# A first graph layer worked on 128x128 matrices, its one-hots on GpSimd, and matmuls that bridge three waits

## The reference

```
x = x + L0_gnn(layernorm(x), emb_1, emb_2, alpha_p, beta_p, edge_weight, src, dst, 5)

def L0_gnn(inputs, emb_1, emb_2, alpha_p, beta_p, edge_vals, edge_row, edge_col, num_iters):
    x1 = inputs @ emb_1
    x2 = inputs @ emb_2
    sim = softmax(leaky_relu(x1 @ x2.T, 0.2), axis=-1)          # 128 x 128
    vals = edge_vals * sim[edge_row, edge_col]                   # 2048 edges
    normalize = segment_sum(vals, edge_row)[:, None]
    alpha, beta = exp(alpha_p), exp(beta_p)
    denom = beta + normalize * alpha + alpha
    for _ in range(num_iters):                                   # out starts as inputs
        sp = segment_sum(vals[:, None] * out[edge_col], edge_row)
        out = (inputs * beta + (sp + out) * alpha) / denom
    return out
```

## Time and profile before

| what | value |
|---|---|
| median of 3 runs | 586.34 us (583.44 to 587.7) |
| profiled execution, own time | 588.12 us |
| its span | 586.4 us |
| mean granted TensorE clock | 0.988 |
| PE busy | 557.6 us, 95% |
| DVE busy | 492.7 us, 84% |
| ACT busy | 413.9 us, 71% |
| POOL busy | 15.7 us, 3% |
| DMA | 168.06 MB, mean 287 GB/s |

### The profile page before, as it was taken

The page is one execution under the profiler, slowest core; times in us unless marked ns, Lnnn a source line. Parts: engine busy times, 40 slices in busy tenths (PEclk is TensorE's granted clock), DMA queues, the critical chain, the costliest instruction groups (busy, mean ns, idle before and its releaser), DMA issues.

```text
span 586.4 us, 8286 instructions
## 1 busy us (share of the span) xinstructions
PE 557.6 (95%) x2743; PEld 453.6 (77%) x2743; DVE 492.7 (84%) x491; ACT 413.9 (71%) x426; POOL 15.7 (3%) x40
## 2 busy tenths in 40 slices
PE   5898999997999999999999999999998799999997
PEld 4666888885678887688888888888877688888886
DVE  7599989886769986888898998989987769998996
ACT  5777787873259876868778778787852457878783
POOL 3100000000100000000000000000000200000000
PEclk9799999998999999999999999999999999999999
DMA  8579998897257975788989989899873158999920
GB/s 285 210 269 424 373 354 343 331 344 267 72 197 285 357 310 190 265 334 336 355 319 352 354 320 355 334 343 352 330 289 118 72 186 308 349 350 365 344 104 19
DMA packets 26861, 168.06 MB, mean 287 GB/s; under 512 B 5228, under 2 KB 5357, under 8 KB 6856
## 3 DMA queue, kind: packets, MB, share of 16 engines
q1 hardware_dynamic: 25430, 165.72, 75.2%
q10 hardware_dynamic: 1410, 2.07, 1.0%
HBM read 167.51 MB, written 0.26 MB: 286 GB/s over the span
## 4 chain that ended last, share of the span: by engine, by line
PE 77%; DVE 11%; ACT 5%; issue 3%; DMA 2%; POOL 2%; ACTq 0%; POOLq 0%; DVEq 0%
PE y L634 33%; PE pre L634 33%; PE tp L646 5%; DVE w_lo L1022 4%; DMA scal<-in_L_gnn_eps 2%; ACT w_hi L366 2%; PE pre L641 2%; DVE st L969 1%; POOL rstd L324 1%; ACT L439 1%; PE wt L867 1%; DVE XN L989 1%; POOL rstd L323 1%; DVE w_lo L1013 0%; DVE X L1107 0%
## 5 line engine op out<-in xcount | busy, mean ns | idle before, releaser
L1022 DVE TENSOR_TENSOR w_lo<-raw,w_hi 128x2048 fp32r<-128x2048 f32 x151 | 340.1, 2287 | 48.7 <-ACT w_hi L366 48.3
L366 ACT ACTIVATE w_hi<-raw 128x2048 fp32r<-128x2048 f32 x152 | 285.4, 1915 | 0.0
L444 ACT ACTIVATE hT_hi<-tp 128x512 fp32r<-128x512 f32 x66 | 39.4, 597 | 82.4 <-PE tp L646 82.4
L634 PE MATMUL pre<-w_hi,x_hi 128*128 128x512 f32 x292 | 81.2, 401 | 0.8 <-ACT x_hi L379 0.7
L634 PE MATMUL pre<-w_lo,x_hi 128*128 128x512 f32 x292 | 79.7, 395 | 2.3 <-DVE w_lo L1013 1.2
L634 PE MATMUL y<-w_hi,hT_hi 128*128 128x512 f32 x280 | 81.7, 413 | 0.0
L634 PE MATMUL pre<-w_hi,x_lo 128*128 128x512 f32 x292 | 78.4, 390 | 0.2
L634 PE MATMUL y<-w_lo,hT_hi 128*128 128x512 f32 x280 | 75.8, 392 | 0.5 <-DVE w_lo L1022 0.4
L634 PE MATMUL y<-w_hi,hT_lo 128*128 128x512 f32 x280 | 75.2, 390 | 0.0
L634 PEld LDWEIGHTS pre<-w_lo,x_hi 128*128 128x128 f32 x292 | 55.5, 191 | 15.7 <-DVE w_lo L1022 2.3
L634 PEld LDWEIGHTS pre<-w_hi,x_hi 128*128 128x128 f32 x292 | 54.9, 192 | 14.2 <-issue 3.5
(11 more groups left out here) (264 smaller groups left out, 395.4 us busy)
## 6 DMA issues: line engine op xcount, KB each, us to landing
raw<-in_chunks SPq DMA_DIRECT2D x156, 1024.0 KB, 5.4
side<-in_L_gnn_emb ACTq DMA_DIRECT2D x1, 512.0 KB, 4.0
affine<-in_L_ffn_W SPq DMA_DIRECT2D x1, 512.0 KB, 7.6
side<-in_L_ffn_W SPq DMA_DIRECT2D x1, 512.0 KB, 10.2
affine<-in_L_gnn_ln_g ACTq DMA_DIRECT2D x2, 256.0 KB, 4.1
affine<-in_L_gnn_ln_b ACTq DMA_DIRECT2D x2, 256.0 KB, 4.6
X<-in_x ACTq DMA_DIRECT2D x1, 256.0 KB, 2.7
affine<-in_L_gnn_gamma SPq DMA_DIRECT2D x1, 256.0 KB, 5.6
```

The source lines that it names most:

```text
L366: act.activation(w_hi[:, g % SPLIT_SLOTS], raw[:, g % RAW_SLOTS], ACT.Copy).then_inc(w_hi_ready, 4)
L444: act.activation(hT_hi[:, (s - 1) % 2], tp[:].rearrange("p (c n) -> p c n", n=P), ACT.Copy).then_inc(hT_hi_ready, 1)
L634: last = pe.matmul(dst, xs[:, k], ws[:, k], start=start and i == 0, stop=stop and i == len(passes) - 1 and bias is None)
L1022: dve.tensor_tensor(w_lo[:, i], raw[:, g % RAW_SLOTS], w_hi[:, i].bitcast(F32), ALU.subtract).then_inc(w_lo_ready, 4)
```

## The change

It has five parts.

1. The edge lists and weights come by one DMA, the three scalars by another, both on SP ahead of the first chunk.
2. POOL builds all 32 plain one-hots: 4 of the sources, then the first layer norm's two steps, then 12 of the sources and 16 of the destinations; behind these the masks, and `sel_all` directly. DVE builds only the 16 weighted ones. ACT builds none, and rounds chunk 0 and 1 earlier; DVE splits two quarters of chunk 0 before it waits for the product x1 x2.
3. The recursion runs on 128x128 matrices: with M1 = A + diag(r), M3 = A A M1 + A diag(r) + diag(r) and the transpose of M5 likewise, the layer's output is one product of M5 with XN, in two column halves.
4. The sum x + out and the statistics behind it are done by column halves.
5. `keep_clock` is added before l1g's turned x (30), and before l3f it is cut in three (15, 33, 14) with a wait for the statistics of l3g_out and l3f between them, in place of 44 at once.

```diff
-BRIDGE = {"l0g": 0, "l0f": 4, "l1f": 37, "l2g": 23, "l2f": 30, "l3g": 28, "l3f": 44}
+BRIDGE = {"l0g": 0, "l0f": 4, "l1g": 30, "l1f": 37, "l2g": 23, "l2f": 30, "l3g": 28, "l3f": 14}
+BRIDGE_L3G_OUT = (15, 33)
+EARLY_SRC = 4
+HOTS_AHEAD = 3
+COUNTS_IN_GAPS = 2
...
+        diag = agg1
+        mat_1 = c_ds
+        mat_3 = mat_a
+        mat_5T = c_sd
...
@@ SP @@
-            for n, name in ((0, "src"), (1, "dst")):
-                sp.dma_start(ends_i[:, n], A[name].rearrange("(p k) -> p k", p=P)).then_inc(sm("edges_in"), 16)
-            sp.dma_start(ends[:, 2], A["edge_weight"].rearrange("(p k) -> p k", p=P)).then_inc(sm("edges_in"), 16)
+            sp.dma_start(ends_i[:].rearrange("p n k -> p (n k)"), A["edges"]).then_inc(sm("edges_in"), 16)
+            sp.dma_start(scal[:], A["scalars"].partition_broadcast(P)).then_inc(sm("scal_in"), 16)
@@ POOL @@
-            link(pool.memset(sel_raw, 0.0))
...
+            def one_hot(dst, n, k):
+                return pool.tensor_scalar(dst[:, k], iota_t[:], ends[:, n, k:k + 1], None, ALU.is_equal)
+            pool.wait_ge(sm("consts"), 1)
+            pool.wait_ge(sm("ends_ready"), 1)
+            for k in range(EARLY_SRC):
+                one_hot(src_hot, 0, k).then_inc(sm("src_ready"), 1)
             inv_std("l0g")
-            pool.wait_ge(sm("hot_ready"), EC)
+            for k in range(EARLY_SRC, EC):
+                one_hot(src_hot, 0, k).then_inc(sm("src_ready"), 1)
+            for k in range(EC):
+                one_hot(dst_hot, 1, k).then_inc(sm("dst_ready"), 1)
...
+            link(pool.memset(flat_sel.bitcast(F32), 0.0))
...
@@ ACT @@
-            act.activation(sel_all[:].rearrange("p e n -> p (e n)"), sel_raw, ACT.Copy).then_inc(sm("sel_all"), 1)
-            for k in range(4):
-                squared_distance(k)
+            act.wait_ge(sm("scal_in"), 16)
+            act.activation(ab[:], scal[:, 0:2], ACT.Exp).then_inc(sm("ab"), 1)
             plain_x("l0g", "xt")
-            for k in range(4, 12):
-                squared_distance(k)
+            round_chunk(0)
...
-            round_chunk(0)
             round_chunk(1)
@@ PE @@
+            weighted_edges(range(HOTS_AHEAD))
             turn_x("l0g")
-            weighted_edges(range(FIRST_HOTS))
+            weighted_edges(range(HOTS_AHEAD, HOTS_AHEAD + 4))
...
-            counted_edges(range(EARLY_COUNTS))
             pe.wait_ge(sm("l0g_a"), 1)
             pe.transpose(ms[:, 0:P], mat_a[:], ident[:]).then_inc(sm("l0g_aT"), 1)
+            count_some(COUNTS_IN_GAPS)
             pe.wait_ge(sm("l0g_aTs"), 1)
             pe.matmul(tp[:, 0:P], mat_a[:], mat_b[:], start=True, stop=True).then_inc(sm("l0g_a2"), 1)
...
-            counted_edges(range(EARLY_COUNTS, EC))
+            pe.wait_ge(sm("l0g_diag"), 1)
+            pe.matmul(pre[1][:, 0:P], mat_b[:], diag[:], start=True, stop=False)
+            pe.matmul(pre[1][:, 0:P], ident[:], diag[:], start=False, stop=False)
+            pe.wait_ge(sm("l0g_m1"), 1)
             pe.wait_ge(sm("l0g_a2s"), 1)
+            pe.matmul(pre[1][:, 0:P], agg2[:], mat_1[:], start=False, stop=True).then_inc(sm("l0g_m3"), 1)
+            pe.matmul(pre[0][:, 0:P], diag[:], mat_b[:], start=True, stop=False)
+            pe.matmul(pre[0][:, 0:P], ident[:], diag[:], start=False, stop=False)
+            pe.wait_ge(sm("l0g_m3s"), 1)
+            pe.matmul(pre[0][:, 0:P], mat_3[:], agg2[:], start=False, stop=True).then_inc(sm("l0g_m5"), 1)
+            count_some(COUNTS_IN_GAPS)
+            pe.wait_ge(sm("l0g_m5s"), 1)
+            for bank_ap, cols in zip((wt[0], tp), COL_HALVES):
+                pe.matmul(bank_ap[:, 0:D // 2], mat_5T[:], XN[:, cols], start=True, stop=True).then_inc(
+                    sm("l0g_out"), 1)
+            count_some(EC)
...
             pe.wait_ge(sm("c_ds"), 1)
+            keep_clock(BRIDGE["l1g"])
...
+            keep_clock(BRIDGE_L3G_OUT[0])
+            pe.wait_ge(sm("var"), nth("var", "l3g_out"))
+            keep_clock(BRIDGE_L3G_OUT[1])
+            pe.wait_ge(sm("var"), nth("var", "l3f"))
             turn_x("l3f")
@@ DVE @@
             for k in range(EC):
-                dve.tensor_scalar(src_hot[:, k], iota_t[:], ends[:, 0, k:k + 1], None, ALU.is_equal)
-                dve.tensor_scalar(weight_hot[:, k], iota_t[:], ends[:, 1, k:k + 1], ends[:, 2, k:k + 1],
+                dve.tensor_scalar(weight_hot[:, k], iota_t[:], ends[:, 1, k:k + 1], edge_weight[:, k:k + 1],
                                   ALU.is_equal, ALU.mult).then_inc(sm("hot_ready"), 1)
-                if k == 0:
+                if k == EARLY_SRC - 1:
                     normalise_x("l0g")
-                if k == SIM_AT:
...
+            split_quarter(0, 0)
+            split_quarter(0, 1)
+            dve.wait_ge(sm("l0g_sim"), 1)
...
+            dve.tensor_scalar(diag[:], ident[:], row[:, 1, 1:2], None, ALU.mult).then_inc(sm("l0g_diag"), 1)
             dve.wait_ge(sm("l0g_aT"), 1)
             dve.tensor_copy(mat_b[:], ms[:, 0:P]).then_inc(sm("l0g_aTs"), 1)
+            dve.tensor_tensor(mat_1[:], mat_a[:], diag[:], ALU.add).then_inc(sm("l0g_m1"), 1)
...
+            dve.tensor_copy(mat_3[:], pre[1][:, 0:P]).then_inc(sm("l0g_m3s"), 1)
+            dve.tensor_copy(mat_5T[:], pre[0][:, 0:P]).then_inc(sm("l0g_m5s"), 1)
+            for part, cols in enumerate(COL_HALVES):
+                dve.wait_ge(sm("l0g_out"), part + 1)
+                link(dve.tensor_tensor(X[:, cols], X[:, cols], (wt[0], tp)[part][:, 0:D // 2], ALU.add))
+                link(dve.bn_stats(st_halves[:, part], X[:, cols]))
+            dve.bn_aggr(mv[:], st_halves[:].rearrange("p a b -> p (a b)")).then_inc(sm("var"), 1)
             normalise_x("l0f")
-            split_quarter(0, 0)
-            split_quarter(0, 1)
             split_quarter(0, 2)
```

More of the change, by code:

```diff
@@ L178, in gnn_ffn_kernel @@
         tri = sb("tri", [P, E8, E8])
-        ends_i = sb("ends_i", [P, 2, EC], I32)
-        ends = sb("ends", [P, 3, EC])
+        ends_i = sb("ends_i", [P, 3, EC], I32)
+        ends = sb("ends", [P, 2, EC])
+        st_halves = sb("st_halves", [P, 2, 6])
         wg0 = sb("wg0", [P, KC, E8])
@@ L344, in _ @@
                                pattern=[[0, 1]], channel_multiplier=-1).then_inc(sm("half"), 1)
+            flat_sel = sel_all[:].rearrange("p e n -> p (e n)")
+            link(pool.memset(flat_sel.bitcast(F32), 0.0))
+            link(pool.affine_select(out=flat_sel, in_=flat_sel.bitcast(F32), compare_op=ALU.not_equal, fill=1.0, base=0,
+                                    pattern=[[-1, E8], [0, P]], channel_multiplier=1))
+            pool.affine_select(out=flat_sel, in_=flat_sel.bitcast(F32), compare_op=ALU.not_equal, fill=1.0, base=-E8,
+                               pattern=[[-1, E8], [0, P]], channel_multiplier=1).then_inc(sm("sel_all"), 1)
             for tag in NORMED[1:]:
@@ L507, in _ @@
             round_x("l0f", True)
+            act.wait_ge(sm("sel_all"), 1)
             pipeline(L0F, lambda: exp_logits("l0f", E8))
@@ L761, in _ @@
             last.then_inc(sm("l0g_x12"), 1)
-            weighted_edges(range(FIRST_HOTS, FIRST_HOTS + 3))
+            weighted_edges(range(HOTS_AHEAD + 4, HOTS_AHEAD + 7))
             pe.wait_ge(sm("l0g_x12s"), 1)
             pe.matmul(ms[:, 0:P], h[:, 0, 0:P], h[:, 0, P:2 * P], start=True, stop=True).then_inc(sm("l0g_sim"), 1)
-            weighted_edges(range(FIRST_HOTS + 3, EC))
-            counted_edges(range(EARLY_COUNTS))
+            weighted_edges(range(HOTS_AHEAD + 7, EC))
+            counts = iter(range(EC))
@@ L767, in _, with count_some @@
+            def count_some(n):
+                counted_edges([k for _, k in zip(range(n), counts)])
             pe.wait_ge(sm("l0g_a"), 1)
             pe.transpose(ms[:, 0:P], mat_a[:], ident[:]).then_inc(sm("l0g_aT"), 1)
+            count_some(COUNTS_IN_GAPS)
             pe.wait_ge(sm("l0g_aTs"), 1)
-            halves = [slice(0, 256), slice(256, 512)]
-            flat_xt = XT[:].rearrange("p c n -> p (c n)")
             pe.matmul(tp[:, 0:P], mat_a[:], mat_b[:], start=True, stop=True).then_inc(sm("l0g_a2"), 1)
-            for part, cols in enumerate(halves):
-                pe.matmul(pre[part][:, 0:256], mat_b[:], XN[:, cols], start=True, stop=True).then_inc(
-                    sm("l0g_sweep"), 1)
@@ L778, in _ @@
-            pe.wait_ge(sm("l0g_rx"), 1)
-            pe.matmul(wt[0][:], mat_b[:], h[:, 1], start=True, stop=True).then_inc(sm("l0g_c2"), 1)
-            pe.wait_ge(sm("l0g_a2s"), 1)
-            for i in range(2):
-                for part, cols in enumerate(halves):
-                    pe.wait_ge(sm("l0g_swept"), 2 * i + part + 1)
-                    pe.matmul(pre[part][:, 0:256], agg2[:], flat_xt[:, cols], start=True, stop=True).then_inc(
-                        sm("l0g_sweep"), 1)
-            counted_edges(range(EARLY_COUNTS, EC))
+            pe.wait_ge(sm("l0g_diag"), 1)
@@ L1454, in _laid_out @@
     arrays["chunks"] = chunks
```

(4 more changed lines are left out.)

54 lines of the change are left out of this document (12 added, 42 removed).

## The result

| | us |
|---|---|
| after, median of 20 runs | 588.83 (587.97 to 589.88) |
| before, median of 20 runs beside it | 586.42 (583.44 to 589.29) |
| ratio after / before | 1.0037, 95% interval 1.0023 to 1.0050 |
| forecast | 582.4 (578 to 587), mostly faster or no change |

The change made the kernel 2.4 us slower. That is less than the 1% I had set as telling, but with 20 runs a side the sign is clear, and it is the other one than forecast. The profiled execution took 587.97 us (span 586.2), against 588.12 for the one of before. It is the fastest of its 20, while that of before lies 1.7 above its median.

The account below looks back on a forecast made before the run. PE was taken to bound the kernel, busy 557.6 of 586.4 us. Terms -3.2 - 0.4 - 1.25 + 1.0 = -3.9 took the profiled 588.12 to 584.2; less 1.8 for the median, 582.4 us, range 578 to 587.

Parts of the forecast that it names:

- I take 0.33: Part 2: each POOL one-hot of 128x128 takes 0.33 us, priced from POOL's select (0.30), within bounds 0.30 and 0.99.
- POOL becomes the bound: Rival, chance 0.08: POOL's list delays l0f's layer norm; at 0.8 per one-hot 592.5 us, at 0.99 598.
- all other gains: The gains outside POOL's list: 0.4, 1.25 and 0.9 of the quarter splits, eaten at 0.61 per one-hot.
- the -3.2: First layer: DVE starts the bias at about 29.3 instead of 32.58, booked as a lasting gain of 3.2 us.
- The page's estimate: POOL one-hot near 0.5 by the skill page: 0.28 for 128 columns beside about 0.2 fixed; kernel at about 584.
- -2.7: First layer: l0f's last statistics done at 25.1 instead of 27.77, 2.0 of the gain from part 2.
- 6.95: First layer norm: XN starts at 6.95 against 6.65 before, +0.3, behind POOL's four one-hots from 4.7 to 6.0.
- 16.75: First layer: matrix A done on DVE at 16.75 instead of 17.74, from +0.3 and -1.3.
- -0.4 - 1.25 = -1.65: Part 5, bridges: -0.4 us at l1g and -1.25 us at l3f, from first products at full clock.
- the forecast's upper bound: POOL and DVE taking turns: 3.7 us, with 2.9 for DVE's one-hots and 0.6 for the quarters; +1.0 was taken.
- The rule of the Trainium skill that I cited: A double-rate tensor_scalar takes GpSimd's interface for the whole instruction, fully blocking the other engine; it spoke against the change.
- The rival of the earlier clock: Rival, chance 0.23: small PE work in the first layer's gaps brings full clock back earlier, giving 579.4 us.

Follow-up runs that it names:

- e5: The changed kernel with POOL writing only 64 of 128 columns of each destination one-hot, a DVE memset filling the rest: 586.06 us, ratio to before 0.9993.
- e2: The changed kernel with 8 of 16 destination one-hots made by ACT and the masks ahead of POOL's eight: 583.83 us, ratio to before 0.9964.
- e9: Against e2, ACT makes 12 of 16 destination one-hots, and PE issues 20 transposes in its wait for A: 583.69 us, ratio to before 0.9956.
- e3: The kernel before with the change's part 5 alone, the bridges at l1g and around l3f: 585.13 us, ratio to before 0.9975.
- e8: The kernel before with the 44 transposes before l3f cut in three and none at l1g: 586.88 us, ratio to before 1.0008.
- e12: The kernel before with the 30 transposes at l1g and nothing else of part 5: 585.13 us, ratio to before 0.9981.
- e10: The kernel before with ten transposes on PE ahead of the first layer's counted matmuls: 585.96 us, ratio to before 1.0003.
- e1: The changed kernel with POOL's masks ahead of the destination one-hots and l0f's two layer norm steps ahead of sel_all: 586.23 us, ratio to before 1.0004.
- e13: e9 with the 44 transposes before l3f at once again, those at l1g kept: 584.41 us, ratio to before 0.9955.

## Why the prediction was wrong

**The step that failed: "I take 0.33, since a comparison of one input is nearest to the select."** It measured 0.609. My bounds, 0.30 and 0.99, held it. The rival "POOL becomes the bound" had the right mechanism, but a chance of 0.08. Its formula gives POOL free at 4.7 + 1.0 + 5.2 + 32 x 0.609 = 30.4; the trace has 30.08. It also said that 0.61 would eat all other gains, so a kernel level with the 588.12 of before; the profiled execution of after took 587.97. DVE came to the bias at 33.61 instead of the 29.3 on which the -3.2 rested. I chose 0.33 although the only arithmetic of POOL in the earlier trace rows, the power on one column, took 0.64. The select was the neighbour by shape, and what decided was another price per column, as e5 shows. Relieving POOL brings 4.3 us by the ratios in e2 and 4.8 in e9 (which holds the clock too), most of the error of 6.4.

**The page's estimate was nearer than mine.** The Trainium skill (GPSIMD Engine Reference, Elementwise — side-by-side cycle accounting) led to an estimate near 0.5. The trace's 0.609 is above that too, and the measurement decides: 2.9 ns a column by e5, against an estimate of 2.2 from the page's figure for two inputs (2.6 cycles at 1.2 GHz).

**The baseline of part 3: -3.2 for the first layer was sized against a half-clock execution.** The earlier trace rows were read rightly, but as a property of the kernel. The first product at 30.25 is that of one execution; e3, e8 and e12 have the same first layer and start at 27.61, 28.29 and 28.71, and e10, with ten transposes more, at 27.44. At full clock the old sweeps take from the copied A (19.02 in e3) to the statistics (25.14) 6.1 us; the small matrices in e9 take from 19.45 to 24.96, 5.5 us. The statistics end at 25.14 in e3, 24.96 in e10 and 24.96 in e9, so most of the -2.7 was the distance from an execution at half clock. The forecast then also subtracted the 1.8 by which that execution lies above the median, and so counted, as far as the two have the same source, one clock loss twice. That source is argued from the table of clocks and not measured. With POOL relieved, the changed first layer brings 0.6 us (e2) to 1.1 us (e9) over e3 by the ratios (0.9964 and 0.9956 against 0.9975, intervals overlapping), so no gain of the size booked is shown.

**Part 2's small terms.** XN of l0g came at 8.02, not at 6.95: POOL's four one-hots took 2.44 and not 1.3. A came at 18.56, not at 16.75. Of these 1.8 us, 1.1 are POOL's. Another 0.3 lies before L1142, where PE now works four weighted groups (1.91 at 9.44) ahead of x1 and x2, to which I had given no time, and 0.4 between L1142 and A.

**Part 5: mechanism right, split wrong.** -0.4 - 1.25 = -1.65 forecast, -1.5 and -1.9 measured by the ratios (-1.1 and -1.3 by the medians), but l1g seems to carry it and l3f next to nothing. l3f's 4.26 in the earlier trace rows was again one execution's.

**Sharing between POOL and DVE: about 0.7, and on POOL's side.** The group of DVE's weighted one-hots in after, and the durations of POOL's (minimum, median and maximum in ns), all 32 and then the two that run between 13 and 14 us, with what DVE did there:

```profile
L1135 DVE TENSOR_SCALAR affine<-iota_t,ends,ends_i 128x128 f32<-128x128 f32 x16 | 4.8, 370 | 0.0
```

```profile
L333 POOL TENSOR_SCALAR raw<-iota_t,ends x32: 597/604/1111, 4.7 to 24.4; 128x128 f32<-128x128 f32 x32
...
L333 POOL TENSOR_SCALAR raw<-iota_t,ends x2: 797/954/1111, 12.1 to 13.2; 128x128 f32<-128x128 f32 x2
```

```profile
12.19 1.37 DVE L1018 TENSOR_TENSOR w_lo<-raw,w_hi 128x512 fp32r<-128x512 f32 x2
```

370 against 338 ns are 0.5 us in all, and hidden. POOL's stay near 0.60 beside them. Two are longer, 1.11 and 0.80, and they fall on DVE's two quarters of w_lo, an operation with two SBUF inputs; e1, e5 and e9 have the same pair there. That is 0.7 us on POOL's list, near the 0.6 that the forecast's upper bound gave the quarters; the 2.9 it gave DVE's one-hots shrank to the 0.5. From 21 to 23, with two short copies on DVE and nothing else, POOL's one-hots took 0.61 all the same, so sharing is not what made them dear. The rule of the Trainium skill that I cited (SBUF — State Buffer, Who interferes with whom) did not show in the short pairs of one-hots. It fits e1's XN, which took 2.25 beside `sel_all`; whether the select blocked it through that interface no run here isolates.

**The rival of the earlier clock** came in part and was undone: half clock lasted from 18.6 to 22 in the first layer, 3.4 us instead of 6.5, but PE's wait of 4.27 for POOL brought a second stretch that before had not. The first follows PE's wait of 2.31 for A and has nothing to do with POOL's lateness; e2's profile has it too (0.76 from 17 to 24). e9 shows that 20 transposes in the first wait keep the clock at 1.00.

## What to carry to other kernels

- Price an operation by the nearest row of the same kind of work on that engine, and if none exists, let the unfavourable end of the bounds carry as much chance as the favourable one when a whole list of 32 hangs on it. Count the list's end before its single terms: at 0.53 an item POOL was ready no earlier than the statistics of before, and at 0.61 all other gains were gone.
- One profiled execution shows one draw of the clock. Before a gain is sized on a stretch at half clock, look whether the run is typical in time and mean clock; if its time is above the median, ask whether it is so in the very stretch that the change touches.
- A helper engine with a long list should have the short steps that others wait for ahead of its bulk, but not right ahead of bulk that disturbs what they start (e1).
- A version that beats both kernels exists: e9_clock_share, 0.9956 of before (0.9934 to 0.9979), 4.8 us below the change by the ratios. e2_share, with one edit less, can't be told from it.

## What the runs showed of the hardware

- POOL's tensor_scalar with is_equal: 0.61 us for 128x128, 0.42 for 128x64, with pointer or constant alike within 0.02 (start to start); its select of 128x128 takes 0.30, and DVE's comparison and multiplication of the same size 0.34.
- POOL and DVE delay each other in both directions where their work coincides: a POOL one-hot took 1.11 instead of 0.60 beside DVE's subtraction of 128x512 with two SBUF inputs (after), and a DVE tensor_scalar of 128x128 took 1.14 instead of 0.28 beside POOL's memset of 128x1024 (e13). Beside DVE's one-hots of 128x128 POOL's kept 0.60.
- The kernel's time falls into steps with the run's mean clock (1.000, 0.994, 0.991, 0.988: 583.0 to 588.6 us). With the waits filled e9 had 7 of 12 runs at 1.000, against none of 11 in e2; e13, with the same first layer, had 2 of 12, and e10 none.
